# The order in which SyncE issues three stacks of attention operands

## What is computed

```python
q, k, v = (_split_heads(q), _split_heads(k), _split_heads(v))
scale = 1.0 / np.sqrt(HEAD_DIM)
L = jnp.einsum('bhqd,bhkd->bhqk', q, k) * scale
mask = jnp.tril(jnp.ones((t, t), dtype=L.dtype))[None, None]
k_y = _split_heads(x @ w_ky.T)
L_y = jnp.einsum('bhqd,bhkd->bhqk', q, k_y) * scale
agg = jnp.sum(jnp.exp(jnp.clip(L_y, -15.0, 15.0)) * mask, axis=-1, keepdims=True) + EPS
r = _eml(L, agg)                      # log(|L| + eps) - log(agg + eps)
w = jax.nn.softplus(r) * mask
A = w / (jnp.sum(w, axis=-1, keepdims=True) + EPS)
out = jnp.einsum('bhqk,bhkd->bhqd', A, v)
```

## Time and profile before

| | |
|---|---|
| median of 3 runs | 466.5 us (465.37 to 467.26) |
| the profiled execution | 465.7 us, of which the span from first to last instruction is 463.9 us |
| TensorE (PE) busy | 330.0 us, 71% |
| VectorE (DVE) busy | 306.6 us, 66% |
| ScalarE (ACT) busy | 285.9 us, 62% |
| GpSimd (POOL) busy | 172.6 us, 37% |
| mean granted clock of TensorE | 0.824 |

### The profile page before, as it was taken

One profiled execution on the slowest core, in us unless ns is written; L12 is line 12 of the kernel. 1 busy time (PEld: TensorE's weight loads), 2 busy tenths in 40 slices (PEclk: granted clock), 3 DMA queues, 4 the chain that ended last, 5 costly groups with the idle time before them and its releaser, 6 DMA issues.

```text
span 463.9 us, 7907 instructions
## 1 busy us (share of the span) xinstructions
PE 330.0 (71%) x2362; PEld 201.8 (44%) x2362; DVE 306.6 (66%) x634; ACT 285.9 (62%) x830; POOL 172.6 (37%) x258
## 2 busy tenths in 40 slices
PE   2817999916677545677968597778879671799991
PEld 1706999803233111212323233234343561689990
DVE  6681222146689979979899999999996748122210
ACT  1204444503789998979899989997775320344550
POOL 6357777411143570014110250106300205777741
PEclk9999999967589655767787779799898655699997
DMA  8716685234563069903000030003001351668530
GB/s 270 212 52 212 199 205 169 76 103 126 154 173 92 0 167 230 231 8 92 2 1 1 1 92 0 3 1 92 1 2 56 104 203 36 210 197 191 159 90 0
DMA packets 38626, 48.85 MB, mean 105 GB/s; under 512 B 4581, under 2 KB 27119, under 8 KB 38332
## 3 DMA queue, kind: packets, MB, share of 16 engines
q1 hardware_dynamic: 33756, 37.67, 29.6%
q0 software_dynamic: 3680, 8.59, 7.1%
q10 hardware_dynamic: 1152, 2.11, 1.4%
HBM read 24.82 MB, written 7.22 MB: 69 GB/s over the span
## 4 chain that ended last, share of the span: by engine, by line
PE 41%; DVE 19%; ACT 15%; issue 9%; DMA 6%; POOL 5%; SPq 4%; POOLq 0%; DVEq 0%
PE PS L1245 11%; PE PS L1229 10%; ACT R L763 6%; DVE R L1054 5%; PE PS L1360 4%; SPq L433 4%; ACT R L771 4%; DMA R<-QPS 3%; ACT CL L763 3%; PE PS L1165 2%; DVE R L1039 2%; PE PS L1342 2%; DVE CL L1039 2%; PE PS L1385 2%; PE PS L1286 2%
## 5 line engine op out<-in xcount | busy, mean ns | idle before, releaser
L1054 DVE TENSOR_TENSOR R<-PS,MB 128x1024 int32<-128x1024 int32 (+1 forms) x96 | 97.8, 1034 | 13.8 <-PE PS L1342 11.3
L679 ACT ACTIVATE R<-PS,R 128x128 f32<-128x128 f32 x184 | 52.4, 368 | 59.1 <-PE PS L1229 59.1
L771 ACT ACTIVATE R<-R 128x1024 f32<-128x1024 f32 x64 | 80.2, 1262 | 10.6 <-DVE R L1054 10.5
L763 ACT ACTIVATE R<-R 128x384 f32<-128x384 f32 (+2 forms) x192 | 77.1, 408 | 8.4 <-DVE R L1039 8.4
L1327 PE MATMUL PS<-R 64*128 64x512 bf16 (+3 forms) x256 | 40.3, 371 | 32.8 <-DVE CL L1039 14.8
L1039 DVE SCALAR_TENSOR_TENSOR R<-PS,MA 128x1024 f32<-128x1024 f32 x64 | 59.6, 947 | 1.3 <-PE PS L1327 0.7
L1360 PE MATMUL PS<-R,V 128*32 128x256 f32 (+3 forms) x512 | 57.0, 534 | 4.6 <-ACT R L771 4.5
L958 DVE SCALAR_TENSOR_TENSOR R<-PS,scoef,R 128x128 f32<-128x128 f32 x46 | 15.9, 350 | 61.6 <-PE PS L1245 61.6
L1229 PE MATMUL PS<-R 128*128 128x128 f32 x368 | 53.1, 291 | 4.1 <-DVE R L949 4.1
L1245 PE MATMUL PS<-R 128*128 x368 | 53.5, 289 | 0.0
L526 POOL DMA_INDIRECT R<-rows_d,R x46 | 44.3, 964 | 22.1 <-issue 18.1
(11 more groups left out here) (164 smaller groups left out, 473.9 us busy)
## 6 DMA issues: line engine op xcount, KB each, us to landing
R<-w SPq DMA_DIRECT2D x38, 258.0 KB
R<-R SPq DMA_DIRECT2D x48, 128.0 KB, 2.4
R<-w SPq DMA_DIRECT2D x2, 2048.0 KB, 10.1
QPS<-R SPq DMA_DIRECT2D x32, 128.0 KB, 2.4
R<-R SPq DMA_DIRECT2D x16, 256.0 KB, 6.5
R<-w ACTq DMA_DIRECT2D x8, 258.0 KB
rows_d<-X SPq DMA_DIRECT2D x8, 256.0 KB, 7.5
rows_d<-R SPq DMA_DIRECT2D x8, 256.0 KB, 3.7
```

The lines of the kernel that those rows point to most:

```text
L679: last = act.activation(HT[:, k % 2, c * P:(c + 1) * P], PS[:, k % 2, c * P:(c + 1) * P], ACT.Gelu, bias=W1[:, k, F + c:F + c + 1])
L763: act.activation(e, e, ACT.Exp, scale=SCALE, accum_out=aggf[:, ds(s + (2 * i + par) * STEPS, 1)])\
L771: act.activation(w, w, ACT.Ln, bias=1.0, scale=1.0).then_inc(s_ln, 1)
L1054: dve.tensor_tensor(weights(v)[:, :, at:at + n].bitcast(i32), PS[:, SLOTS[slot(b_fill(v, g))], 0:n].bitcast(i32), spread(mask, 1, 2), ALU. ...
```

## The change

SyncE's order was stacks 0 to 5, scaled queries of batch 0, stacks 8, 7, 6, scaled queries of batches 1 to 3. It becomes stacks 0 to 7, scaled queries of batch 0, stack 8, scaled queries of batches 1 to 3. No instruction is added or taken away, and the waits of each stack go with it.

```diff
-            for i in range(6):
+            for i in range(8):
                 stack(i)
             scaled_q_stack(0)
-            for i in (8, 7, 6):
-                stack(i)
+            stack(8)
             for b in range(1, NB):
                 scaled_q_stack(b)
```

## The result

In the first comparison the changed kernel took 461.1 us (459.92 to 461.67, 4 runs) and the kernel before 466.59 (465.37 to 467.26, 4 runs). The ratio is 0.9882 with an interval of 0.9853 to 0.9911: 5.5 us less, 4.2 to 6.9 by the interval. The profiled execution took 460.87 us, its span 459.1 (before: 465.7 and 463.9).

The account below looks back on a forecast made before the run. The prediction took TensorE's wait at step 16 for stack 6's late DMA, which left VectorE idle, as the bound. Gains of 3.32 and 0.2 us made 3.5, so 466.5 became 463.0 us, range 461.4 to 465.5.

Parts of the forecast that it names:

- The mechanism: Stacks 6 and 7 issued in SyncE's hole before 164.09 us, so TensorE's 4.64 us DMA wait at step 16 goes.
- The signs of being wrong: TensorE at step 12 after 172.5; waits for ScalarE, 198 to 210 us; VectorE's gaps, 205 to 345, 2 us longer.
- The gain at VectorE: Step 16: VectorE reaches `abs_scores(4, 0)` at 196.67 us instead of 199.99, a gain of 3.32.
- The second gap: VectorE's gap before `abs_scores(4, 1)` at step 16 goes from 0.55 to 0.35 us, 0.2 more gained.
- The sum to `abs_scores(4, 1)`: VectorE's two gains at step 16 together: 3.5 us, between 3.3 and 3.9.
- The price at the scaled queries: Step 12: scaled queries land 0 to 0.3 us later for TensorE; 1.5 us of cover behind GpSimd, so costed at 0.
- ScalarE: Around step 16: would not hold VectorE up, costed at 0; if it bound, the gain would be 1.4 to 2.9 us.
- the last one, from the sum to the two medians: Whole kernel: the profiled execution's 3.5 us saving applied to the median of 466.5 us, giving 463.0.
- Rival 2: The busier stretch around step 16 keeps TensorE's clock high: gain 4.4 to 5.5 us, 461.5; chance 11%.
- Theory B: The stall costs more than its gap, as TensorE's clock falls in it and later steps wait: 5 to 6 us.

Follow-up runs that it names:

- experiment 2: Kernel before with only stack 6 put ahead of the scaled queries, stacks 8 and 7 behind them: 462.0 us, ratio 0.9937.
- the second execution: Another profiled execution of the unedited changed kernel, from the comparison that measured 462.29 us (12 runs) against 465.43 (35 runs).
- experiment 4: Kernel before with 16 unread matmuls on TensorE ahead of its wait for stacks 6 and 7: 464.72 us, ratio 0.9992.
- experiments 1 and 3: 1: changed kernel again, no edit, ratio 0.9931. 3: kernel before with 3 or 12 added DMAs ahead of stack 6, ratios 1.0008 and 1.0122.
- e10_yardstick: The changed kernel, no edit, against the kernel before on another chip: 509.02 us against 512.8, ratio 0.9936.
- e8: Changed kernel with unread TensorE matmuls in both feed-forwards, 12 and 13 ahead of the slot indices, 9 and 12 behind them: ratio 0.994.
- e11: Changed kernel with unread matmuls, 13 and 14 ahead of the slot indices, 18 and 21 behind, 4 and 1 behind the first two transposes: ratio 0.9927.

## Why the forecast was wrong, point by point

**The mechanism** held. The stacks are issued in the hole, the wait at step 16 is gone, nothing new stands in its place, and experiment 2 shows that the wait alone is what counts. The signs of being wrong stayed away: from 198 to 210 us neither VectorE nor TensorE waits for L770 or L762, and VectorE's gaps from 205 to 345 us (202 to 342 in the changed kernel) are 6.6 us in sum and 5.4 in the second execution, against 5.2 before, so less than 2 us longer.

**The gain at VectorE**, 3.32 for the first gap: 3.32 in both executions (2.93 + 0.39 and 2.86 + 0.46). The second gap, worked out as 0.35, is 0.37. The sum to `abs_scores(4, 1)`: 202.81 - 199.78 + 0.39 = 3.42 against 3.5.

**The price at the scaled queries**, 0 to 0.3 us on TensorE: 0.24, and 0.43 in the second execution (171.92, with 0.46 of offset). It was covered in both, as VectorE's 2.35 and 2.33 behind GpSimd show. **ScalarE** didn't bind: its logarithms of pair 4 start at 200.24, 0.02 off what the forecast had with the offset, and VectorE waits for it nowhere from step 12 to 16.

**The term that failed is the last one, from the sum to the two medians.** The forecast took 466.5, a median of 3 runs, as the kernel's time, and made its range, 461.4 to 465.5, out of mechanisms only. It put the spread of the runs at nothing there, though it had said itself that a measurement tells about 2.3 us from no change. Over 35 runs the kernel before takes 465.43 on a chip of nearly this speed and the changed one, over 12, takes 462.29. Measured by that chip, 466.6 was 1.2 high and 461.1 was 1.2 low: 2.4 of the 5.5 us, and the rest is 3.2. No more runs were made on the chip of the first comparison, so this split is an inference. The profiled pair shows the like: of its 4.8 us, 3.4 less the offset of 0.4 are won by the end of the stall, and 1.8 behind it, where TensorE's clock differs. A kernel whose single runs have a standard deviation of 1.3 to 1.7 us has a median of 4 with about half of that on either side, and the difference of two such medians needs some 2 us more at either end of the range. It had 1.6 below the forecast, all of it given to rival 2. What could have said so was there: three runs of one kernel 1.9 us apart.

**Rival 2** (the clock helps too) is nearest to the time of the first comparison, with its 461.5, and the profiled execution shows 4.8 won at the end instead of 3.0. But its mechanism, a stall that keeps the clock low, did not show: the changed kernel has a granted clock of 0.50 at this place too and `weigh` takes its 1.93, the second execution wins next to nothing behind the stall (0.1), and experiment 4 puts the high clock at 0.55 us at this step. Theory B, made after the result to explain 5.5, fell with experiments 1 and 3 and the yardstick.

## What to carry to other kernels

When a DMA queue's backlog ends an engine's wait, look for the hole in the issuing engine's timeline ahead of the urgent copies, and move into it what is ready; what it wins is the gap on the engine that binds, read at that engine and not at the one that waits for the DMA (3.3 and not 4.6). Before a forecast of under 1%, take the spread of the runs shown as a term of its own: three runs 1.9 us apart do not fix a time to better than a microsecond. And lay two executions of one kernel side by side before explaining a difference between two kernels.

## What the runs showed of the hardware that I had not expected

- SBUF copies of 256 KB in this pattern drain at 1.12 us each (233 GB/s in the earlier trace rows), where the copies of the same size to HBM added 0.54 (3 of them) and 0.67 us (12 of them) each to the stall.
- One kernel's time differs by 47 us between chips (465.4 and 512.8), while its attention takes the same: VectorE's instructions of 1.21 to 1.23 us are so on both. Two stretches hold it. Of the changed kernel, the second pass's `abs_scores(0, 0)` starts on VectorE at 173.52 us on the one and at 197.02 on the other (e10_yardstick), 23.5 later; the second routing's first maximum at 372.46 and 394.16, no further apart; and a copy at the start of the second feed-forward at 399.37 and 442.64, 43.3 apart. In the first, VectorE's sum of slot coefficients starts at 63.87 us on the slower chip, 24.90 after the instruction ahead of it, and at 41.66 on the other. It starts again 3.9 us after the last of GpSimd's gathers (59.95), which run through most of the wait; in the second feed-forward the same instruction waits 22.4 us and starts 0.9 after them. The cause stays open.
- A fill can raise TensorE's clock and still be of no use: in e8, 9 added matmuls ran in 2.10 us, at 2.4 GHz; then TensorE idled for 2.49 us, did one transpose, idled for 1.30 more, and the first group took 2.08 us, at 1.2. In e11, with 18 matmuls there and 0.56 us of idling behind them, 4 more behind the transpose and again 0.56, the group took 1.16, at 2.4.
